# Attention's output product from rounded high and low parts, queries and keys in four places instead of five

## The reference, cut to what matters

```python
dots = jnp.einsum('bhid,bhjd->bhij', q, k) * SCALE
m = jax.nn.softmax(dots, axis=-1)
diag = jnp.diagonal(m, axis1=-2, axis2=-1)
...
keep = jnp.abs((diag - mu) / sd) <= Z_THRESH
valid = keep[..., :, None] & keep[..., None, :]
masked = jnp.where(valid, dots, NEG)
attn = jax.nn.softmax(masked, axis=-1)
...
out = jnp.einsum('bhij,bhjd->bhid', attn, v)
out = out.transpose(0, 2, 1, 3).reshape(b, n, h * d)
return out @ w_out.T + b_out
```

## Time and profile before

| | us |
|---|---|
| median of 3 runs | 1904.43 (1904.3 to 1905.6) |
| time of the profiled execution | 1905.04 |
| its span, first to last instruction | 1903.5 |
| attention, about | 710 to 1777 |
| TensorE busy over the whole span | 1787.5 (94%) |

### The profile page before, as it was taken

One profiled execution on the slowest core, in us unless ns is written; L12 is line 12 of the kernel. 1 busy time (PEld: TensorE's weight loads), 2 busy tenths in 40 slices (PEclk: granted clock), 3 DMA queues, 4 the chain that ended last, 5 costly groups with the idle time before them and its releaser, 6 DMA issues. The chain is left out here.

```text
span 1903.5 us, 29906 instructions
## 1 busy us (share of the span) xinstructions
PE 1787.5 (94%) x11064; PEld 1216.9 (64%) x11064; DVE 1326.4 (70%) x2493; ACT 1149.2 (60%) x1715; POOL 1172.5 (62%) x660
## 2 busy tenths in 40 slices
PE   8998999888999897899999999999999999999888
PEld 5883444334785663577777777777777777765466
DVE  5627899986335764667677777777777767778676
ACT  6326777853435546666766676767676776653554
POOL 5551767874453551277777676777767777777354
PEclk9999999999999998899999999999999999999999
DMA  2000000000001002221212221221212121200100
GB/s 99 1 1 1 1 0 1 1 0 1 0 1 50 1 7 69 56 65 48 60 47 60 48 60 47 59 61 46 71 36 71 47 60 47 57 24 12 50 6 17
DMA packets 43664, 66.03 MB, mean 35 GB/s; under 512 B 24768, under 2 KB 26176, under 8 KB 43264
## 3 DMA queue, kind: packets, MB, share of 16 engines
q1 hardware_dynamic: 43056, 63.54, 13.1%
q10 hardware_dynamic: 432, 0.59, 0.1%
q0 software_dynamic: 32, 0.00, 0.0%
HBM read 29.05 MB, written 1.24 MB: 16 GB/s over the span
## 5 line engine op out<-in xcount | busy, mean ns | idle before, releaser
L2410 POOL TENSOR_TENSOR at_e_lo<-at_e,at_e_hi 128x1024 fp32r<-128x1024 f32 x256 | 612.9, 2394 | 304.2 <-DVE at_e_hi L2385 297.2
L2167 ACT ACTIVATE at_e<-at_ps,at_dropped 128x1024 f32<-128x1024 f32 x256 | 285.7, 1116 | 216.4 <-PE at_ps L1880 200.6
L2264 DVE CUSTOM_DVE_ANT_0 at_ps<-at_ps,at_mask 128x1024 f32<-128x1024 f32 x256 | 313.4, 1224 | 7.3 <-PE at_ps L2000 4.9
L2159 ACT ACTIVATE at_ps<-at_ps,at_neg_diag 128x1024 f32<-128x1024 f32 x256 | 278.6, 1088 | 49.1 <-DVE at_neg_diag L2255 48.7
L2385 DVE CAST at_e_hi<-at_e 128x1024 fp32r<-128x1024 f32 x256 | 228.3, 892 | 23.6 <-ACT at_e L2167 20.4
L1959 PE MATMUL at_ps<-at_kq,at_qk 64*128 64x512 f32 x768 | 226.3, 403 | 12.3 <-DMA at_kq<-at_qk 10.5
L1960 PE MATMUL at_ps<-at_qk,at_kq 64*128 64x512 f32 x768 | 226.4, 403 | 0.0
L2009 PE MATMUL at_ps<-at_qk,at_kq 64*128 64x512 f32 x768 | 224.7, 399 | 1.6 <-DVE at_row_max L2264 1.1
L1880 PE MATMUL at_pv_ps<-at_e_hi,at_v_hi 64*128 64x512 f32 x980 | 225.6, 453 | 0.3 <-issue 0.2
L2010 PE MATMUL at_ps<-at_kq,at_qk 64*128 64x512 f32 x768 | 224.6, 398 | 0.0
L1056 POOL TENSOR_TENSOR mb_work<-mb_work,mb_c 128x1024 f32<-128x1024 f32 x64 | 151.8, 2372 | 96.5 <-DVE mb_work L1025 94.2
(11 more groups left out here) (392 smaller groups left out, 4162.9 us busy)
## 6 DMA issues: line engine op xcount, KB each, us to landing
at_kq<-at_qk SPq DMA_DIRECT2D x128, 256.0 KB, 3.9
at_mask<-at_mask_dram SPq DMA_DIRECT2D x32, 256.0 KB, 3.7
at_recips<-at_recip_row SPq DMA_DIRECT2D x31, 256.0 KB, 4.5
ffn_h_raw<-in_h SPq DMA_DIRECT2D x2, 1024.0 KB, 7.5
at_head_w_raw<-in_w_qkv SPq DMA_DIRECT2D x32, 64.0 KB, 3.9
x<-in_x SPq DMA_DIRECT2D x4, 256.0 KB, 4.9
moe_gate_in<-in_gate_in SPq DMA_DIRECT2D x2, 512.0 KB, 3.8
moe_up_in<-in_up_in SPq DMA_DIRECT2D x2, 512.0 KB, 4.5
```

The costliest lines, as they stand in the source:

```text
L2159: act.eng.activation(ps[:], ps[:], ACT.Exp, scale=SCALE, bias=m.small["neg_diag"][s][:, blk:blk + 1], accum_out=m.small["sums"][s][:, blk: ...
L2167: act.eng.activation(m.e[e % 2][:], slot("turned_scores", h, blk)[:], ACT.Exp, scale=SCALE, bias=m.small["dropped"][h % SLOTS][:, blk:blk ...
L2264: dve.eng.tensor_tensor_reduce(out=ps[:], in0=ps[:], in1=m.mask[h % 2][:], scale=1.0, scalar=-BIG, op0=ALU.add, op1=ALU.max, accum_out=m.s ...
L2410: pool.eng.tensor_tensor(m.e_lo[e % 3][:], m.e[e % 2][:], m.e_hi[e % 3][:].bitcast(F32), ALU.subtract).then_inc(sem["at_lo"])
```

## The change

The output weights are rounded once, at the start of attention, into a high part (ScalarE) and a low part (GpSimd). For each head up to 29, ScalarE rounds the head's half of `heads_out` into a high part, in the step `AT_NORM` behind its other work, and GpSimd makes the low part in the step after, behind that step's `e_lo`. The output product becomes three fp32r products in place of one in float32; only the last head's stays float32. Head 29's product now also goes through `project_out`. The counts of the semaphore `at_norm` are changed to match, since it now counts two events for each head. `SLOTS`, the number of places for queries and keys (and for the small tiles of a head), goes from five to four.

```diff
-SLOTS = 5
+SLOTS = 4
...
+PAIRED = NH - 2
...
+def normed(h):
+    return min(2 * h + 1, 2 * PAIRED + 1)
...
     act.eng.activation(m.wv_hi[:], m.wv_raw[:], ACT.Copy).then_inc(sem["at_wv_hi"])
+    act.eng.activation(m.w_out_parts[0][:], m.w_out[:], ACT.Copy).then_inc(sem["at_wv_hi"])
...
     pool.eng.tensor_tensor(m.wv_lo[:], m.wv_raw[:], m.wv_hi[:].bitcast(F32), ALU.subtract).then_inc(sem["at_wv_lo"])
-    pool.wait_ge(sem["at_wv_lo"], 1)
+    pool.wait_ge(sem["at_wv_hi"], 2)
+    w_hi, w_lo = m.w_out_parts
+    pool.eng.tensor_tensor(w_lo[:], m.w_out[:], w_hi[:].bitcast(F32), ALU.subtract).then_inc(sem["at_wv_lo"])
+    pool.wait_ge(sem["at_wv_lo"], 2)
...
-            pe.wait_ge(sem["attn_out_load"], 16)
-            pe.wait_ge(sem["at_norm"], h + 1)
+            pe.wait_ge(sem["at_wv_lo"], 2)
+            pe.wait_ge(sem["at_norm"], normed(h) + 1)
             slot_free(pe, c, m, "out", h)
-        mm = both_rows([ps[:, half] for half in HALF], m.w_out[:, pair, :], [m.heads_out[:, half] for half in HALF],
-                       not turned, turned, turned)
+        (w_hi, w_lo), (hi, lo) = m.w_out_parts, m.heads_parts
+        for n, (w, x) in enumerate(((w_hi, hi), (w_lo, hi), (w_hi, lo))):
+            mm = both_rows([ps[:, half] for half in HALF], w[:, pair, :], [x[:, half] for half in HALF],
+                           n == 0 and not turned, n == 2 and turned, turned)
...
             if (h := pair_due(t)) is not None:
-                if apart:
+                if h != LAST:
                     project_out(h, turned)
...
+    def round_heads(h):
+        place = slice(HD, P) if h % 2 else slice(0, HD)
+        act.wait_ge(sem["at_norm"], normed(h))
+        if h >= 2:
+            act.wait_ge(sem["at_out"], h // 2)
+        act.eng.activation(m.heads_parts[0][place, :], m.heads_out[place, :], ACT.Copy).then_inc(sem["at_heads_hi"])
...
         if at := due(t, AT_MEAN):
             deviations(at[0])
+        if (at := due(t, AT_NORM)) and at[0] < PAIRED:
+            round_heads(at[0])
...
             if h:
-                pool.wait_ge(sem["at_norm"], h)
+                pool.wait_ge(sem["at_norm"], min(2 * h, 2 * PAIRED + 1))
             if h >= 2:
-                pool.wait_ge(sem["at_out"], h // 2)
+                pool.wait_ge(sem["at_heads_hi"], h - 1)
             pool.eng.tensor_tensor(m.heads_out[place, :], m.pv_sb[0:HD, :], m.recips[:],
                                    ALU.mult).then_inc(sem["at_norm"])
+        if (at := due(t, AT_NORM + 1)) and at[0] < PAIRED:
+            h = at[0]
+            place = slice(HD, P) if h % 2 else slice(0, HD)
+            hi, lo = m.heads_parts
+            pool.wait_ge(sem["at_heads_hi"], h + 1)
+            pool.wait_ge(sem["at_lo"], min(t - AT_TURNED + 1, NH * BLK))
+            pool.wait_ge(sem["at_w_lo"], min((t - AT_SPLIT) // BLK + 1, NH))
+            pool.eng.tensor_tensor(lo[place, :], m.heads_out[place, :], hi[place, :].bitcast(F32),
+                                   ALU.subtract).then_inc(sem["at_norm"])
```

More of the change, by code:

```diff
@@ L68 @@
     "moe_w_hi", "moe_xn_hi", "moe_scores", "moe_silu", "moe_comb_hi", "moe_hi",
-    "at_wv_hi", "at_xn_hi", "at_qk_hi", "at_v_hi", "at_sum", "at_dev", "at_exp", "at_pv_out",
+    "at_wv_hi", "at_xn_hi", "at_qk_hi", "at_v_hi", "at_sum", "at_dev", "at_exp", "at_pv_out", "at_heads_hi",
 )
@@ L2079, in project_out_alone @@
         pe.wait_ge(sem["attn_out_load"], 16)
-        pe.wait_ge(sem["at_norm"], min(h + 1, LAST))
+        pe.wait_ge(sem["at_norm"], normed(LAST - 1))
         slot_free(pe, c, m, "out", h)
@@ L2203, in attention_act @@
             if h:
-                act.wait_ge(sem["at_norm"], h)
+                act.wait_ge(sem["at_norm"], normed(h - 1))
             if h < LAST:
@@ L2323, in last_norm @@
             dve.wait_ge(sem["at_pv_out"], LAST + 2 * hf + 2)
-            dve.wait_ge(sem["at_norm"], LAST)
+            dve.wait_ge(sem["at_norm"], normed(LAST - 1))
             dve.eng.tensor_tensor(step, m.pv_ps[HD:, HALF[hf]], inv, ALU.mult).then_inc(done)
@@ L2393, in norms_before @@
     def norms_before(t):
-        return min(max(t - AT_NORM + BLK - 1, 0) // BLK, LAST)
+        normed = min(max(t - AT_NORM + BLK - 1, 0) // BLK, LAST)
+        return normed + min(max(t - AT_NORM - 1 + BLK - 1, 0) // BLK, PAIRED)
     for t in range(AT_FIRST, AT_LAST):
@@ L2437, in attention @@
         m.w_out = sb("at_w_out", [P, HEADS // 2, P])
+        m.w_out_parts = [sb(f"at_w_out_{part}", [P, HEADS // 2, P], F32R) for part in ("hi", "lo")]
         m.xn_hi = sb("at_xn_hi", [P, TOK], F32R)
@@ L2471, in attention @@
         m.heads_out = sb("at_heads_out", [P, SEQ])
+        m.heads_parts = [sb(f"at_heads_{part}", [P, SEQ], F32R) for part in ("hi", "lo")]
         m.small = {k: [sb(f"at_{k}{i}", [P, BLK]) for i in range(SLOTS)] for k in
```

## The result

The changed kernel takes 2071.2 us, the median of 4 runs (2069.43 to 2072.75), beside 1904.37 for the kernel before (1903.09 to 1905.6): 1.0875 times as long, 95% interval 1.0859 to 1.0891, 167 us more. The forecast was 2080, so it is 9 us under it and well inside the range.

What follows compares the result with a forecast made beforehand. TensorE's work and, nearly level, the chain projection, `round_qk`, LO, `best` bound attention. Wait 108 + clock 57 + last heads 14 - product 3 = 176 us, giving 2080 us; 8-in-10 range 2028 to 2122.

Steps and rivals of the forecast that it cites:

- the wait, 27 gaps: ScalarE's copy waits for GpSimd's multiplication, so `round_qk` and `best` come 4.0 us later in 27 heads: 108 us.
- the clock, 27 heads: TensorE's granted clock falls behind each new gap, costing 2.1 us a head: 57 us.
- GpSimd's low part, steady heads: GpSimd's added subtraction, 2.4 us a head behind `e_lo`, fits in the step and costs nothing.
- last heads: Heads 27 to 29: exponentials held on ScalarE and the low part on GpSimd's chain cost 14 us, bounds 7 and 20.
- output product: Three fp32r pairs a half take 1.38 for 1.61 us, 0.23 less a product, 3.2 us for 14; bounds 0 and 4.8.
- Rival 3: ScalarE isn't held, as GpSimd's multiplication is done in time; only the product changes, 1901 us; chance 0.05.
- rival 1: TensorE's clock stays up, or its falls lie in the gaps: 2023 us, up to 2040; chance 0.18.
- Rival 2: GpSimd's two instructions in a row shut VectorE out, 0.7 us more if the clock is up; worst 2140 us, chance 0.13.
- A gain on TensorE counts in full: TensorE's own work bounds attention, so any time saved there, as in the output product, shortens the kernel by as much.
- Four places, the rounding of `w_out`: SLOTS four for five, and ScalarE's 1.04 us rounding of `w_out` ahead of 3.74 us idle: both cost nothing.
- Rival 4: The output product is no shorter in parts, so only its 3 us are gone: 2083 us; within the forecast's chance of 0.64.

Runs made afterwards that it cites:

- wait_only: Kernel before plus one wait, no work: ScalarE, last in step AT_NORM of heads 0 to 29, waits for GpSimd's multiplication; 2018.63 us, ratio 1.0597.
- gap_filled: Changed kernel with TensorE repeating the scores' three pairs five more times in the gap's step of heads 0 to 26; 2049.48 us, ratio 1.0758.
- round_later: Changed kernel with ScalarE's copy two steps later (AT_NORM + 2) and GpSimd's low part behind it (AT_NORM + 3); 1974.82 us, ratio 1.0369.
- product_only: round_later with ScalarE's copy and GpSimd's low part both cut to 16 of 1024 columns, product's twelve instructions kept; 1906.07 us, ratio 1.0007.
- in_holes: Changed kernel, heads from 26 on as before, ScalarE's copy and the low part (on VectorE) at AT_NORM + 8, product at AT_OUT 51; 1909.02 us, ratio 1.0017.

## Why the prediction was right, and which of its terms were not

| term | forecast, us | measured, us |
|---|---|---|
| the wait, 27 gaps | 108 | 27 x 4.02 = 109 |
| the clock, 27 heads | 57 | 950.3 - 931.5 = 19, and 2 in head 26 |
| GpSimd's low part, steady heads | 0 | 26 x 0.95 = 25 |
| last heads | 14 | 12 |
| output product | -3 | none in the time |
| sum | 176 | 167 |

**The wait: right, step by step.** ScalarE's copy waits 4.63 to 4.65 us in 26 of the 27 heads and 4.92 in one (forecast 4.6), takes 1.05, and `round_qk` starts 1.11 or 0.99 after the multiplication's end, in turn (forecast 1.01). Counted as in the prediction, from the last pair's start plus 0.23, `best` stands for 4.20 to 4.36, and once 4.50 (forecast 4.26). From the gap before of 0.27, that is 4.02 a head in the mean. `wait_only` shows the cause: a wait with no work behind it gives 114 us, its own falls of the clock included. Rival 3 is out.

**The clock: the mechanism right, the size wrong.** It falls at every gap, and at most 1.6 us of a low stretch lie in the gap, so rival 1 as it stood is out. But the step "What it costs is between 1.53 and twice that ... I take 2.1" read the loss of one step from the earlier trace rows and took it as a loss of time for every head. It is that only where TensorE alone sets the pace. With the clock up, `gap_filled` waits for VectorE's row maximum in every second head, and what the falls cost on top is 22 us in all, 0.8 a head: nothing for a fall of 3.4 us, and 0.9 or 2.35 for one of 6.8. Where GpSimd does less, as in `wait_only`, it is some 1.1, worked out by subtraction; no run separates it there. Nor was a fall certain, as nine gaps of `wait_only` show.

**GpSimd's low part: this step was wrong.** "It fits, if barely. If that cover went, I price it below." It does not fit. The page of before has GpSimd busy 62%, but its time is not free to be used: the low part holds up both the next `e_lo` and the next rounding on VectorE. In the changed kernel:

```profile
1114.23 2.40 POOL L2453 TENSOR_TENSOR at_heads_lo<-at_heads_out,at_heads_hi 64x1024 fp32r<-64x1024 f32 x1
...
1115.53 1.66 DVE L2406 CAST at_e_hi<-at_e 128x1024 fp32r<-128x1024 f32 x1
```

Rival 2 had the mechanism, with 0.7 us a head if the clock is up; it is 0.95, and in the place of `round_later` 2.05. Rival 2 also says that with the clock down TensorE comes later and doesn't notice; two of four heads of `gap_filled` fit that. So the two terms overlap: in the sum, the clock's was 36 too large and this one's 25 too small. That the forecast stands only 9 us off is in part luck: these two errors nearly cancel.

**The product: too small a gain on TensorE, and none in the time.** After, it takes 0.68 and 0.69 a half, as forecast. But 3.57 - 3.20 makes the float32 product 1.38 + 0.37 = 1.75, not 1.61: the 0.57 taken for a plain step holds 0.11 of its own beside two pairs at 0.23. So the gain was 0.37 x 14 = 5.2 us, over the bound of 4.8. The four passes of the Trainium skill's page "FP8 and Floating Point Precision", section "TensorE Precision Notes", give an estimate of 1.84 (eight pairs at 0.23), and 1.75 lies nearer to that. And "A gain on TensorE counts in full" failed in `product_only`: that before shows TensorE hardly waiting for the row maximum did not say how near to it the row maximum was.

**The last heads.** 133.5 - 114.6 = 18.9, less head 26's own 6.5 (39.2 for 32.7), is 12.4 (forecast 14). **Four places, the rounding of `w_out`.** Nothing. The new copy of `w_out` takes 1.04, and ScalarE idles 2.77 us behind it in place of 3.74. Rival 4 is out by the product's rows.

## What to carry to other kernels

A wait for a fresh result costs what stands behind it in its engine's queue, and a wait with no work does so as well: put the instruction where its engine was idle anyway and its input is an old one, which here, with the low part moved to another engine and the last four heads left in float32, took 167 us down to 3. Don't read an engine's idle share as room: read the idle stretch in the place itself, and what the neighbour engine does in it. And once one engine's delay has made another's as late, remove them both before you price either; the terms of such a sum overlap.

## What the runs showed of the hardware

- VectorE's subtraction of two SBUF operands, 64 x 1024, stands while GpSimd reads: 2.33 us under `e_lo`, 1.08 of it after `e_lo`'s end; and in `in_holes` GpSimd's multiplication took 3.19 for 2.4 behind it. The Trainium skill's page "SBUF — State Buffer", section "Who interferes with whom", says that a VectorE instruction with two SBUF inputs contends with a GpSimd instruction that reads SBUF. The runs agree, both ways round.
- Size is no shelter: a 128 x 8 operation on VectorE took 1.80 us under `e_lo`, where its mean before is 0.30.
- A GpSimd subtraction of 64 x 16 still takes 0.55 to 0.66 us in the mean, where 64 x 1024 takes 2.4.
- Repeated matmuls into a place that is overwritten behind them kept the granted clock at 1.00 through the steady stretch, where it was 0.93 without them; it paid back 22 us of 167.
- The granted clock fell behind idle stretches of TensorE of 1.38 to 1.84 us in `round_later`, ten times, and did not fall at nine of the 27 stretches of 3.11 us in `wait_only`. The length of one wait did not tell whether the clock would fall.
